# Expert rows by indirect DMA instead of by products with one-hot matrices

## The chip, the core and the metric

The program runs on one core of one Trainium2 chip. The metric is the device time of one execution in microseconds (us), lower being better. Engine names are those of the profile: PE (TensorE matmul), PEld (its weight load), DVE (VectorE), ACT (ScalarE), POOL (GpSimd), SP (SyncE); SPq and ACTq are the DMA issues of SP and ACT.

## What is computed

One transformer layer over 32 x 64 = 2048 rows of 128 elements: cross attention with a distance bias, then a mixture of 8 experts.

```python
x = x + xattn(layernorm(x), ctx, ctx, positions, ...)       # 16 heads of 8
xf = layernorm(x).reshape(-1, 128)
gate_logits = selu(xf @ gate_wi + gate_bi) @ gate_wo + gate_bo     # [2048, 128]
topv, topi = top_k(gate_logits, 2); topv = topv / topv.sum(-1)
onehot = (topi[..., None] == arange(8))                      # most of the 128 places name no expert
w = einsum('nk,nke->ne', topv, onehot)
h = selu(einsum('nh,ehf->enf', xf, exp_wi) + exp_bi)         # [8, 2048, 512]
out_e = einsum('enf,efh->enh', h, exp_wo) + exp_bo
x = x + einsum('enh,ne->nh', out_e, w)
```

The two chosen places are among 128, and only places 0 to 7 are experts, so that few rows have an expert at all.

## The kernel before

Rows lie in 16 tiles of 128 (`T`), in 4 groups of 4 (`TG`). Attention goes through the tiles. Then the second normalisation makes `XN2` (ACT `norm2`, DVE L889 for the last group; `inverse_std` on POOL, L383), and the gate goes through groups g and chunks c: PE `hidden(g, c)` (L1206), ACT exp and relu (L627, L628), DVE `SG` (L875), PE `logits(g)` (L1254), DVE adds, maxima and their places (L839 to L850). Each engine's order is written out by hand, and semaphores join the engines.

Beside that, every group of `XN2` is split into three bf16 parts that sum to the float32 value: ACT `first_part` (L584), POOL `rest2` (L402), ACT `second_part` (L588), POOL `last2` (L408). They go to `XW`, with three bf16 parts of the row's weights for the 8 experts and the membership (0 or 1) behind them.

The expert stage then works by products with one-hot matrices:

- DVE `choose` (L855) makes memberships and `Ub` (has the row any expert). PE counts (L1276 to L1278), and DVE turns counts into two loop bounds and ranks (L913 to L922).
- `pick_candidates` (L924) makes one-hots `G1` of up to 32 candidate rows of each tile. PE multiplies `XW` by `G1` (L1314) to give the candidates' rows and weights, `XC`, 4 blocks (`NC`) of 128.
- From prefix counts (`places`, L1294) comes `slot`: at which of the 128 places (`CAP`) of an expert a candidate stands. DVE makes the one-hots `G2` (L956), 4 x 1024 columns.
- PE multiplies `XC` by `G2` (L1324, 24 matmuls of 512 columns) for the transposed rows `XG` of all experts. Weights of the places come from L1379. `G1` and `G2` are transposed on PE (L1306, L1334) and copied out (L654, L965).
- For each expert PE `hidden(e)` (L1342), ACT and DVE selu (L677, L679, `selu` L967), PE `output(e)` (L1346): the expert's bias by one matmul (L1356) and four products (L1358; each float32 matmul shows as two records).
- Weighted outputs are split in three bf16 parts (`weigh` L661, `weigh_rest` L977). PE brings them back by `GT2` (`scatter`, L1362), DVE splits the sums again (L1010 to L1014), PE brings them to rows by `GT1` (L1403), DVE adds to `X` (L1019), and SP stores the four groups (L375).
- `expert_corrections` (L1235) makes a correction of the experts' bias rows: half of it right after the last logits, half after the counts.

The two loops around this run as often as the counts ask for; with these inputs each runs once.

Of the kernel before, what the change touches and what calls it, by code (L numbers as in the profile page):

```python
# [16 lines left out]
F32 = mybir.dt.float32  # L17
# [7 lines left out]
P = 128  # L25
# [5 lines left out]
CAND = 32  # L31
# [3 lines left out]
def build(nc, x, ctx_in, pos, Wq, bq, Wk, bk, Wv, bv, Wo, bo, emb, g_wi, g_bi, g_wo, g_bo, e_wi, e_bi, e_wo, e_bo, out):  # L35
# [23 lines left out]
    XWW = 3 * D + 4 * E  # L59
# [4 lines left out]
    with st:  # L64
# [6 lines left out]
        def sem(name):  # L71
            return st.enter_context(nc.semaphore(name))


        bins_dram = dram("bins_dram", [T, JB, IB, 2, L], BF16)
# [7 lines left out]
        ones_row = sb("ones_row", [2, P], F32)  # L83
# [12 lines left out]
        ebo_rows = sb("ebo_rows", [2, E, D], F32)  # L96
# [12 lines left out]
        ab = ExitStack()  # L109
        posq = sb("posq", [P, T, 3], F32, ab)  # L110
        posT = sb("posT", [T, P * 3], F32, ab)
        CX = XN2
        early = XW[:, :, :].rearrange("p t w -> p (t w)").bitcast(F32)
# [5 lines left out]
        w_att = sb("w_att", [P, 4, D], F32, ab)  # L119
        brow = ebo_rows[0:1, 0:5, :]  # L120
        bcols = sb("bcols", [P, 4], F32, ab)
        bo_b = sb("bo_b", [P, D], F32, ab)
# [5 lines left out]
        OH = sb("OH", [P, 2, IB * P], BF16, ab)  # L128
        bin_f = sb("bin_f", [P, 1], F32, ab)
# [25 lines left out]

        G1 = sb("G1", [P, T, P], BF16)
        GT1 = sb("GT1", [P, T, P], BF16)
        XC = sb("XC", [P, NC, XWW], BF16)
        OC = sb("OC", [P, NC, D], F32)
        OCr = sb("OCr", [P, NC, D], F32)  # L160
        OC3 = sb("OC3", [P, 3, NC, D], BF16)
        G2 = sb("G2", [P, NC, SLOTS], BF16)

        XN2T = sb("XN2T", [P, T * P], F32)
# [18 lines left out]
        GT2 = sb("GT2", [P, NC, E, P], BF16)  # L183
# [8 lines left out]
        Yr = sb("Yr", [P, 2, 2, D], F32)  # L192
        Y3 = sb("Y3", [P, 3, E, D], BF16)
# [6 lines left out]
        YB = [OPS, MPS, PTP[1], OPS]  # L200
        NY = len(YB)
        SCB = [PTP[0], SPS[0]]
        BKB = [SPS[1], SPS[2], SPS[3], SPS[0]]
# [5 lines left out]
        d_posq, oh_done, posq_tr, posq_done, bias_tr, perm_done, s_first, s_mm, pool_c, d_out = map(sem, (  # L209
            "d_posq", "oh_done", "posq_tr", "posq_done", "bias_tr", "perm_done", "s_first", "s_mm", "pool_c", "d_out"))  # L210
# [4 lines left out]
        xt_ev, q_ev, ge_done, d_gate, d_eb, d_ew, ao_tr, wo_mm = map(sem, (  # L215
            "xt_ev", "q_ev", "ge_done", "d_gate", "d_eb", "d_ew", "ao_tr", "wo_mm"))
        aot_ev, sub_done, exp_done, pv_mm, p_tr, pt_ev, n2_tr, n2_ev = map(sem, (
            "aot_ev", "sub_done", "exp_done", "pv_mm", "p_tr", "pt_ev", "n2_tr", "n2_ev"))
        consts2, h_mm, sg_done, cnt_done, xc_mm, xc_ev, g1_tr, xg_mm = map(sem, (
            "consts2", "h_mm", "sg_done", "cnt_done", "xc_mm", "xc_ev", "g1_tr", "xg_mm"))  # L220
        xg_ev, g2_tr, gt2_ev, eh_mm, se_done, he_done, dve_c = map(sem, (
            "xg_ev", "g2_tr", "gt2_ev", "eh_mm", "se_done", "he_done", "dve_c"))
# [4 lines left out]
        hr_done, y_mm, yb_done, y3_done, sc_mm, xw_done, eb_mm, eb_row = map(sem, (  # L227
            "hr_done", "y_mm", "yb_done", "y3_done", "sc_mm", "xw_done", "eb_mm", "eb_row"))
        mem_mm, mem_ev, y0_done, yr_done, gt1_ev, g1_zero, vs_done = map(sem, (
            "mem_mm", "mem_ev", "y0_done", "yr_done", "gt1_ev", "g1_zero", "vs_done"))  # L230
        w3_done, f_done, gb_mm, gb_ready, back_mm, rsum_done, stats_done, rstd_done = map(sem, (
            "w3_done", "f_done", "gb_mm", "gb_ready", "back_mm", "rsum_done", "stats_done", "rstd_done"))
        var2_done, shift_done, p0_done, p1_done, x2r_done, pool_const, dve_const, d_late = map(sem, (
            "var2_done", "shift_done", "p0_done", "p1_done", "x2r_done", "pool_const", "dve_const", "d_late"))
        WARM, IDENT, PART, KEYS, VD_ONES, NOUGHT, CONSTS = range(1, 8)
        VD_ZERO, BIASES, WQ_SCALED, BD_READY = 1, 2, 3, 3 + JB
        oc3_done = [sem(f"oc3_done{half}") for half in range(2)]
# [6 lines left out]
        x_back = [sem(f"x_back{q}") for q in range(NC)]  # L244
# [16 lines left out]
        out_dram = out.rearrange("b l d -> (b l) d").rearrange("(t p) d -> p t d", p=P)  # L261
# [19 lines left out]
        def _(sp):  # L281
# [69 lines left out]
            for t in range(4, T):  # L351
# [15 lines left out]
                if t == 2 * TG + 1:  # L367
                    sp.dma_start(ebi[:, :, :], e_bi.rearrange("e (c p) -> p e c", p=P), allow_slow_non_contiguous=True).then_inc(d_eb, 16)
                    sp.dma_start(ebo_rows[1:2, :, :], e_bo.rearrange("(a e) h -> a e h", a=1)).then_inc(d_eb, 16)

            sp.wait_ge(cnt_done, 1)
            outer = sp.value_load(cnt_i[0:1, 0:1], min_val=1, max_val=P // CAND)
            for g in range(NG):
                sp.wait_ge(x_back[g], outer)
                sp.dma_start(out_dram[:, tiles(g), :], X[:, tiles(g), :]).then_inc(d_out, 16)  # L375
            sp.wait_ge(d_out, 16 * NG)

        @block.gpsimd
        def _(pool):
# [18 lines left out]

            def rest2(g):

                pool.wait_ge(p0_done, g + 1)
                nc.gpsimd.tensor_tensor(x2r[:, :, :], XN2[:, tiles(g), :], XW[:, tiles(g), 0:D], ALU.subtract).then_inc(x2r_done, 1)  # L402

            def last2(g):

                pool.wait_ge(x2r_done, g + 1)
                pool.wait_ge(p1_done, g + 1)
                nc.gpsimd.tensor_tensor(XW[:, tiles(g), 2 * D:3 * D], x2r[:, :, :], XW[:, tiles(g), D:2 * D], ALU.subtract).then_inc(xw_done, 1)  # L408
                pool.wait_ge(xw_done, g + 1)
# [34 lines left out]
            link(nc.gpsimd.memset(ones_row[:, :], 1.0 / SELU_SCALE))  # L444
# [15 lines left out]
            pool.wait_ge(mv2_done, T)  # L460
            nc.gpsimd.memset(G1[:, :, :].rearrange("p t n -> p (t n)").bitcast(F32), 0.0).then_inc(g1_zero, 1)
# [7 lines left out]
            w3 = [XW[:, :, 3 * D + s * E:3 * D + (s + 1) * E] for s in range(3)]  # L469
# [3 lines left out]
            nc.gpsimd.tensor_tensor(w3[2], Wr[:, :, :], w3[1], ALU.subtract).then_inc(w3_done, 1)  # L473

        @block.scalar
        def _(act):
# [105 lines left out]
            def first_part(g):  # L582
                act.wait_ge(n2_done, g + 1)
                nc.scalar.activation(XW[:, tiles(g), 0:D], XN2[:, tiles(g), :], ACT.Copy).then_inc(p0_done, 1)  # L584

            def second_part(g):
                act.wait_ge(x2r_done, g + 1)
                nc.scalar.activation(XW[:, tiles(g), D:2 * D], x2r[:, :, :], ACT.Copy).then_inc(p1_done, 1)  # L588

# [6 lines left out]
            for t in range(T):  # L596
# [14 lines left out]
                if t in (TG + 2, 2 * TG + 2, T - 1):  # L611
                    norm2(t // TG - 1)
                    first_part(t // TG - 1)
                if t in (TG + 3, 2 * TG + 3):
                    second_part(t // TG - 1)
# [4 lines left out]
            for g in range(NG):  # L620
                for c in range(FC):
# [9 lines left out]
                    if c == FC - 2 and g < NG - 1:  # L631
                        evac_n2(g + 1)
                    if g == 0 and c == FC - 1:
                        second_part(NG - 2)

                if g == 1:
                    first_part(NG - 1)
                if g == 2:
                    second_part(NG - 1)
# [788 lines left out]
```

## Time and profile before

| | us |
|---|---|
| median of 3 runs | 216.96 |
| lowest and highest run | 215.62, 220.72 |
| profiled execution | 216.22 |
| its span, first to last instruction | 214.5 |

The profile is of one execution, so sums are made against its span of 214.5, which lies 1.72 us under that execution's own time. Attention takes roughly the first 128 us of the span, the gate the time to about 163, and the expert stage the rest. A timeline row gives start, length, engine, line, operation, output<-input, shape and count; brackets give the idle time of the engine before the row and what ended it.

### The profile page before, as it was taken

What the parts mean: (1) busy time and instruction counts of PE and PEld (TensorE: products, weight loads), DVE (VectorE), ACT (ScalarE), POOL (GpSimd) and SP (SyncE); (2) the same over time, 40 slices, a digit from 0 to 9 for tenths busy, and PEclk for the clock granted to TensorE, in tenths of its full rate; (3) what the DMA queues carried; (4) which work ended last, traced back from release to release, by engine and by line L of the source; (5) the groups of instructions that cost most, each with busy time, mean ns of one, the idle gap of its engine ahead of it and who ended that gap; (6) DMA issues with size and microseconds to landing.
All of it is one profiled execution on the core that took longest, in us unless ns stands there. A gap on an engine that the chain in (4) does not pass through costs nothing.

```text
span 214.5 us, 6218 instructions
## 1 busy us (share of the span) xinstructions
PE 185.8 (87%) x2516; PEld 139.5 (65%) x2517; DVE 160.7 (75%) x409; ACT 112.9 (53%) x225; POOL 43.8 (20%) x59
## 2 busy tenths in 40 slices
PE   2788839887999999999999997999995799999961
PEld 2355518475977767777777754758770449988951
DVE  6489995899977796779687735666899755788484
ACT  3278863543344376436744689597701245876100
POOL 7353998000000204020302001420303200000000
PEclk9999996999699999999999999999999999999999
DMA  5983599218994878996000000000000000000006
GB/s 137 261 206 105 115 361 394 76 38 280 286 314 128 255 137 212 367 392 218 3 3 3 3 0 0 2 5 0 2 0 0 3 0 3 2 3 2 0 3 196
DMA packets 28005, 24.20 MB, mean 113 GB/s; under 512 B 8628, under 2 KB 22215, under 8 KB 27976
## 3 DMA queue, kind: packets, MB, share of 16 engines
q1 hardware_dynamic: 25944, 23.01, 35.9%
q10 hardware_dynamic: 2032, 0.79, 1.4%
q8 instruction: 20, 0.33, 0.6%
q14 instruction: 9, 0.07, 0.1%
HBM read 17.24 MB, written 1.31 MB: 86 GB/s over the span
## 4 chain that ended last, share of the span: by engine, by line
PE 44%; DVE 30%; ACT 11%; issue 6%; POOL 3%; DMA 2%; SPq 1%; DVEq 1%; ACTq 0%; POOLq 0%
PE pair L1122 8%; PE pair L1136 6%; PE pair L1161 5%; PE pair L1149 5%; PE pair L1358 4%; PE pair L1342 4%; DVE mx L810 3%; DVE PR L813 2%; ACT GR L628 2%; ACT GE L627 2%; PE pair L1324 2%; DVE i L850 2%; PE pair L1368 2%; DMA ebo_rows<-in_L_xattn_bv_dram 2%; ACT PR L598 2%
## 5 line engine op out<-in xcount | busy, mean ns | idle before, releaser
L1122 PE MATMUL pair<-BD,OH 128*128 128x64 bf16 x768 | 27.3, 199 | 3.1 <-DVE OH L728 2.7
L1122 PEld LDWEIGHTS pair<-BD,OH 128*128 128x128 bf16 x768 | 26.7, 102 | 4.8 <-DVE BD L802 3.5
L598 ACT ACTIVATE PR<-PR 128x1024 f32<-128x1024 f32 x16 | 16.9, 1056 | 24.1 <-DVE PR L813 24.1
L605 ACT ACTIVATE PT<-pair 128x512 f32<-128x512 f32 x32 | 17.5, 595 | 16.9 <-PE pair L1149 16.8
L810 DVE TENSOR_REDUCE mx<-pair 128x16 f32<-128x1024 f32 x16 | 19.3, 1208 | 3.1 <-PE pair L1136 3.0
L1136 PE MATMUL pair<-KD,QT 64*64 64x256 f32 x256 | 21.4, 409 | 0.1
L383 POOL TENSOR_TENSOR rstd<-vare,half_neg 128x4 f32<-128x4 f32 x8 | 9.0, 1131 | 60.9 <-DVE vare L762 51.5
L1161 PEld LDWEIGHTS pair<-VD,PT 128*64 128x64 f32 x512 | 16.3, 138 | 6.3 <-issue 6.3
L813 DVE TENSOR_TENSOR PR<-pair,mx 128x1024 f32<-128x1024 f32 x16 | 19.6, 1224 | 0.5
L1149 PE MATMUL pair<-ident,PR 128*128 128x128 f32 x128 | 17.4, 280 | 2.7 <-ACT PR L598 2.3
L1149 PEld LDWEIGHTS pair<-ident,PR 128*128 128x128 f32 x128 | 14.3, 142 | 5.8 <-ACT PR L598 5.0
L1161 PE MATMUL pair<-VD,PT 128*64 128x18 f32 x512 | 17.9, 212 | 0.0
L875 DVE SCALAR_TENSOR_TENSOR SG<-GE,GR 128x512 f32<-128x512 f32 x16 | 10.8, 690 | 6.5 <-ACT GR L628 6.4
L1206 PE MATMUL pair<-XN2T,w_gi 128*128 128x512 f32 x32 | 15.0, 599 | 0.6 <-ACT XN2T L594 0.6
L1254 PE MATMUL pair<-w_go,SG 128*128 128x128 f32 x128 | 15.0, 276 | 0.5 <-issue 0.5
L1254 PEld LDWEIGHTS pair<-w_go,SG 128*128 128x128 f32 x128 | 14.7, 192 | 1.1 <-issue 1.1
L740 DVE TENSOR_TENSOR X<-X,pair 128x128 f32<-128x128 f32 x16 | 4.6, 286 | 14.3 <-PE pair L1175 14.2
L627 ACT ACTIVATE GE<-pair,gb_exp 128x512 f32<-128x512 f32 x16 | 11.4, 711 | 4.4 <-DVE SG L875 4.4
L728 DVE TENSOR_SCALAR OH<-BB,bin_id 128x2048 bf16<-128x2048 bf16 x16 | 13.2, 829 | 0.0
L628 ACT ACTIVATE GR<-pair,gbi 128x512 f32<-128x512 f32 x16 | 11.5, 716 | 0.0
L677 ACT ACTIVATE he<-pair,eb_exp 128x128 f32<-128x128 f32 x32 | 9.2, 374 | 4.3 <-PE pair L1342 4.3
L402 POOL TENSOR_TENSOR x2r<-XN,XW 128x512 f32<-128x512 f32 x4 | 4.6, 1162 | 32.0 <-ACT XW L584 32.0
(201 smaller groups left out, 352.0 us busy)
## 6 DMA issues: line engine op xcount, KB each, us to landing
BB<-bins_dram SPq DMA_DIRECT2D x16, 512.0 KB, 6.8
KD<-x2r SPq DMA_DIRECT2D x2, 2048.0 KB, 10.3
w_ei<-in_L_ffn_exp_wi_dram SPq DMA_DIRECT2D x8, 256.0 KB, 5.9
w_eo<-in_L_ffn_exp_wo_dram SPq DMA_DIRECT2D x8, 256.0 KB, 7.0
w_ei<-in_fside_BxSx_dram SPq DMA_DIRECT2D x8, 192.0 KB, 4.5
X<-in_x_dram SPq DMA_DIRECT2D x4, 256.0 KB, 6.4
KD<-KT SPq DMA_DIRECT2D x32, 32.0 KB, 2.5
out_dram<-X SPq DMA_DIRECT2D x4, 256.0 KB, 2.9
```

Of the source, the lines that this page charges most:

```text
L598: nc.scalar.activation(PR[:, t % 2], PR[:, t % 2], ACT.Exp).then_inc(exp_done, 1)
L605: nc.scalar.activation(PT[:, t % 2, 4 * half:4 * half + 4, :].rearrange("p c n -> p (c n)"), PTP[half][:, :], ACT.Copy).then_inc(pt_ev, 1)
L627: nc.scalar.activation(GE[:, n % 2, :], SPS[n % 4][:, :], ACT.Exp, bias=gb_exp[:, c:c + 1])
L628: nc.scalar.activation(GR[:, n % 2, :], SPS[n % 4][:, :], ACT.Relu, bias=gbi[:, c:c + 1]).then_inc(ge_done, 1)
L810: link(nc.vector.reduce_max(mx[:, t % 2], rows, AX.XY))
L813: nc.vector.tensor_tensor(PR[:, t % 2].rearrange("p h (i k) -> p h i k", i=2), rows, mx[:, t % 2].unsqueeze(2).unsqueeze(3).broadcast_to([ ...
L1122: mm(o, OH[:, t % 2, i * P:(i + 1) * P], BD[:, s], start=(i8_ == 0 and s == 0), stop=False, skip_group_check=True)
L1136: last = mm(SPS[two + ih][b2 * L:(b2 + 1) * L, r * JH * L // 2:(r + 1) * JH * L // 2], QT[rows, g, q0:q0 + L], KD[rows, g % KBUF, :, q0 + ...
L1149: last = tr(PTP[half][:, c * P:(c + 1) * P], PR[:, t % 2, 2 * cc:2 * cc + 2, :].rearrange("p h k -> p (h k)"), ident[:, :])
L1161: last = mm(OPS[b2 * L:(b2 + 1) * L, c * VW:(c + 1) * VW], PT[:, t % 2, c, b2 * L:(b2 + 1) * L], VD[:, 2 * t + b2, c, :], start=True, stop ...
L1206: mm(SPS[n % 4][:, :], w_gi[:, c * P:(c + 1) * P], XN2T[:, GTOK * g:GTOK * (g + 1)], start=True, stop=True).then_inc(h_mm, 1)
L1254: last = mm(o[:, u * D:(u + 1) * D], SG[:, g % 2, c, u * P:(u + 1) * P], w_go[:, c, :], start=(c == 0), stop=(c == FC - 1))
```

## The change

- The normalised rows `XN2` are stored to a DRAM tensor `x2_dram` as soon as each group is made. The rows after attention, `X`, are stored to the output early too, group by group. Both from SP, in the time of attention and gate.
- The bf16 parts of the rows and their four helpers are gone. `XW` now holds 3 parts of the weights, 2 labels (partition number, 128 times the tile number) and the membership.
- Ranks and slots of non-members are not sent far away but behind the members (`turn`, `minus_bf`, `past`), so that every one of the 128 places of an expert names a different row, of weight 0 if it is no member.
- `G2` is made in four batches of two experts (`pick_slots`). After each, PE sums weights and labels of the places (`sums_of_slots`), and DVE makes the row numbers (`rows_of_slots`, `row_i`).
- POOL fetches each expert's 128 rows of 512 bytes with an indirect DMA from `x2_dram` to `XR`; PE transposes them (`rows_transposed`); ACT or DVE copies them to `XG`.
- Each expert's weighted output goes by an indirect DMA that adds, from `Yw` to the output in DRAM. POOL waits for each of these eight before it issues the next.
- All transposes of one-hots, `scatter`, L1403 and L1019 are gone. The bias matmul has 128 rows in place of 2 (the others zero), and the bias corrections stand between the slot batches.

```diff
-            for g in range(NG):
-                sp.wait_ge(x_back[g], outer)
+            for g in range(NG):
+                sp.wait_ge(n2_done, g + 1)
+                sp.dma_start(x2_dram.rearrange("(t p) d -> p t d", p=P)[:, tiles(g), :], XN2[:, tiles(g), :]).then_inc(d_rows, 16)
+                sp.wait_ge(x2_done, TG * (g + 1))
                 sp.dma_start(out_dram[:, tiles(g), :], X[:, tiles(g), :]).then_inc(d_out, 16)
...
             for g in range(NG):
                 pool.wait_ge(var2_done, g + 1)
                 inverse_std(g)
-                rest2(g)
-                last2(g)
...
+            with pool.Fori(0, outer) as ro:
+                with pool.Fori(ro * inner, ro * inner + inner) as k:
+                    for b in range(NB2):
+                        pool.wait_ge(rows_done, k * NB2 + b + 1)
+                        pool.sem_inc(pool_seen, 1)
+                        for e in range(EB * b, EB * b + EB):
+                            pool.indirect_dma_start(XR[:, e, :], None, x2_dram, bass.IndirectOffsetOnAxis(row_i[:, e:e + 1], 0),
+                                                    bounds_check=B * L - 1).then_inc(d_xr[e], 16)
+                    for e in range(E):
+                        pool.wait_ge(y_done, k * E + e + 1)
+                        pool.sem_inc(pool_seen, 1)
+                        pool.indirect_dma_start(out_rows, bass.IndirectOffsetOnAxis(row_i[:, e:e + 1], 0), Yw[:, e, :], None,
+                                                bounds_check=B * L - 1, compute_op=ALU.add).then_inc(d_scat, 16)
+                        pool.wait_ge(d_scat, k * (16 * E) + 16 * (e + 1))
+                        pool.sem_inc(pool_seen, 1)
...
 # ACT, in the inner loop, ahead of the experts
+                    for b in range(2):
+                        act.wait_ge(xr_tr, k * NB2 + b + 1)
+                        nc.scalar.activation(XG[:, b * EB * CAP:(b + 1) * EB * CAP], PTP[0][:, 0:EB * CAP], ACT.Copy).then_inc(xg_ev, 1)
...
 # DVE
+            link(nc.vector.tensor_tensor(rank[:, :], rank[:, :], MPS[:, T * E + 2 * T:T * E + 3 * T], ALU.mult))
-                olink(nc.vector.memset(OC[:, :, :], 0.0))
+                    for b in range(NB2):
+                        pick_slots(b)
+                        rows_of_slots(b)
...
+                    for e in range(2, E):
                         selu(e)
+                        weigh(e - 2)
+                        if e in (2, 4):
+                            evac_xg(1 + e // 2)
+                    weigh(E - 2)
+                    weigh(E - 1)
+                    dve.wait_ge(d_scat, k * (16 * E) + 16 * E)
+                dve.wait_ge(xc_mm, ro + 1)
                 pick_candidates()
...
 # PE
-            expert_corrections(0)
...
+                    sums_of_slots(0)
+                    expert_corrections(0)
+                    sums_of_slots(1)
+                    expert_corrections(1)
+                    sums_of_slots(2)
+                    sums_of_slots(3)
+                    rows_transposed(0)
                     hidden(0)
                     hidden(1)
+                    rows_transposed(1)
                     for e in range(2, E + 2):
                         if e < E:
                             hidden(e)
+                        if e in (2, 4):
+                            rows_transposed(1 + e // 2)
                         output(e - 2)
```

The new `rows_of_slots(b)` is three DVE instructions on 2 experts (a sum of labels, a cast to integers, a sum of weights), and `weigh(e)` is one DVE multiplication of 128x128 from PSUM into `Yw`, which releases `y_done`.

## Rows read from the trace of the kernel before

**Rows 1.** Page, busy time of each engine, and the chain that ended last.
```profile
PE 185.8 (87%) x2516; PEld 139.5 (65%) x2517; DVE 160.7 (75%) x409; ACT 112.9 (53%) x225; POOL 43.8 (20%) x59
PE 44%; DVE 30%; ACT 11%; issue 6%; POOL 3%; DMA 2%; SPq 1%; DVEq 1%; ACTq 0%; POOLq 0%
```

**Rows 2.** Windows: stretch, length, PE, PEld, DVE, ACT, POOL busy, PEclk, DMA.
```profile
178.45:201.10 22.65, 22.63 (x220) 20.67 (x221) 16.33 (x42) 14.72 (x54) 0.00 (x0) 1.00 0.01 2
204.45:214.50 10.05, 3.67 (x60) 3.15 (x57) 6.91 (x18) 0.00 (x0) 0.00 (x0) 1.00 0.36 104
```

**Rows 3.** Chain that ended last, one expert's turn: start, us, what.
```profile
184.75 0.89 PE pair L1342 x8
185.65 0.41 PE pair L1356 x2
186.06 1.09 PE pair L1358 x8
```

**Rows 4.** Timeline, the end of the span.
```profile
201.11 0.62 ACT L668 ACTIVATE Y<-pair,wsl 128x128 bf16<-128x128 f32 x2 [3.67 <-PE pair L1358]
208.98 2.34 SPq L375 DMA_DIRECT2D out_dram<-X  x4
210.98 0.89 DVE L927 TENSOR_TENSOR G<-rank,slot_iota 128x128 bf16<-128x128 f32 x4 [0.23 <-DVE X L1019]
```

**Rows 5.** Timeline, gate: last norm, last logits, memberships.
```profile
134.45 1.16 POOL L408 TENSOR_TENSOR XW<-x2r,XW 128x512 bf16<-128x512 f32 x1 [4.79 <-ACT XW L588]
136.80 1.12 DVE L889 TENSOR_SCALAR XN<-X,mv,rstd 128x128 f32<-128x128 f32 x4 [2.09 <-POOL rstd L383]
155.90 3.81 PE L1254 MATMUL pair<-w_go,SG 128*128 128x128 f32 x32 [0.46 <-issue]
163.39 0.29 DVE L864 TENSOR_REDUCE Ub<-XW 128x16 bf16<-128x128 bf16 x1
```

**Rows 6.** Timeline, ranks and slots.
```profile
168.03 0.48 DVE L944 MEMSET OC<- 128x512 f32 x1 [0.17 <-PE pair L1291]
168.55 0.19 DVE L946 CAST memc<-pair 128x32 bf16<-128x32 f32 x1
168.80 0.23 PE L1298 MATMUL pair<-memc,ones_bf 128*128 128x24 bf16 x3 [0.45 <-DVE memc L946]
169.57 4.63 DVE L956 TENSOR_TENSOR G<-slot,slot_iota 128x1024 bf16<-128x1024 f32 x4 [0.21 <-DVE slot L951]
```

**Rows 7.** Timeline, from the slots to the first expert.
```profile
177.34 1.09 ACT L659 ACTIVATE XG<-pair 128x512 f32<-128x512 f32 x2 [3.06 <-PE pair L1324]
178.47 1.16 PE L1342 MATMUL pair<-XG,w_ei 128*128 128x128 f32 x8
179.47 0.98 PE L1379 MATMUL pair<-XC,G 128*128 128x3 bf16 x32
179.67 1.14 ACT L677 ACTIVATE he<-pair,eb_exp 128x128 f32<-128x128 f32 x4 [1.25 <-PE pair L1342]
182.24 0.69 DVE L974 SCALAR_TENSOR_TENSOR SE<-he,hr 128x512 f32<-128x512 f32 x1
```

**Rows 8.** Output tensor by tile, and POOL's rest of rows by line: landing, duration.
```profile
DMA to landing us min/median/max: 2.4/2.9/3.3
L402 POOL TENSOR_TENSOR x2r<-XN,XW x4: 1158/1162/1165, 80.8 to 142.4; 128x512 f32<-128x512 f32 x4
```

**Rows 9.** DMA issues: output<-input, queue, count, KB each, us to landing.
```profile
bins_dram<-binv ACTq DMA_DIRECT2D x2, 32.0 KB, 2.2
```

**Rows 10.** Windows and PE timeline around an idle PE; columns as above.
```profile
30.00:32.00 2.00, 0.00 (x0) 0.00 (x0) 1.93 (x7) 0.66 (x2) 1.83 (x3) 1.00 1.05 409
34.00:35.00 1.00, 1.00 (x9) 0.24 (x9) 1.00 (x3) 0.00 (x0) 1.00 (x1) 0.50 1.05 385
32.34 1.66 PE L1122 MATMUL pair<-BD,OH 128*128 128x64 bf16 x48 [2.72 <-DVE OH L728]
```

**Rows 11.** Groups by form, 162 to 178.4: busy us, mean ns, idle before.
```profile
L1239 PE MATMUL pair<-w_eo,neg_alpha 128*1 128x512 f32 x4 | 1.9, 591 | 0.0
L1291 PE MATMUL pair<-XW,G 128*128 128x8 bf16 x16 | 0.6, 167 | 1.5 <-DVE G L927 1.5
```

More of the change, by code:

```diff
@@ L58, in build @@
     NC = T * CAND // P
-    XWW = 3 * D + 4 * E
+    XWW = 6 * E
+    MEMB = 5 * E
+    SUMS = 5
+    EB = 2
+    NB2 = E // EB
     MAXRI = T * CAND // CAP
@@ L443, in _ @@
             nc.gpsimd.memset(neg_alpha[:, :], -SELU_ALPHA)
-            link(nc.gpsimd.memset(ones_row[:, :], 1.0 / SELU_SCALE))
+            link(nc.gpsimd.memset(ones_row[:, :], 0.0))
+            link(nc.gpsimd.memset(ones_row[0:2, :], 1.0 / SELU_SCALE))
             nc.gpsimd.memset(ones_row[0:1, :], 1.0)
@@ L468, in _ @@
             link(nc.gpsimd.tensor_tensor(Wt[:, :, :], we[:, 0], we[:, 1], ALU.add))
-            w3 = [XW[:, :, 3 * D + s * E:3 * D + (s + 1) * E] for s in range(3)]
+            w3 = [label(s) for s in range(3)]
             link(nc.gpsimd.tensor_copy(w3[0], Wt[:, :, :]))
@@ L632, in _ @@
                         evac_n2(g + 1)
[L633 to L639, printed above, removed]
-            for i in range(2):
-                act.wait_ge(eb_mm, i + 1)
-                nc.scalar.activation(ebo_rows[0:1, 4 * i:4 * i + 4, :].rearrange("a e h -> a (e h)"), SPS[2 + i][0:1, :], ACT.Copy).then_inc(eb_row, 1)
             act.wait_ge(consts2, 2)
@@ L680, in _ @@
                         last.then_inc(he_done, 1)
-                        if e % 2 == 1 and e >= 3:
-                            weigh((e - 3) // 2)
-                    weigh(NY - 1)
         @block.vector
@@ L997, in _ @@
                     dve.wait_ge(wsl_done, k + 1)
[L998 removed]
                     selu(0)
[L1000 to L1001 removed]
+                    selu(1)
+                    for e in range(2, E):
                         selu(e)
[L1003 to L1014 removed]
@@ L1301, in places @@
                        skip_group_check=True).then_inc(slot_mm, 1)
-                def g1_transposes(half):
-                    pb = PTP[half][:, :].bitcast(BF16)
-                    for u in range(T // 2):
-                        last = tr(pb[:, u * P:(u + 1) * P], G1[:, half * (T // 2) + u, :], ident_bf[:, :])
-                    last.then_inc(g1_tr, 1)
-                g1_transposes(0)
                 places()
@@ new lines, in _, with sums_of_slots @@
+                    pe.wait_ge(xc_ev, ro + 1)
+                    def sums_of_slots(b):
+                        pe.wait_ge(g2_done, k * NB2 + b + 1)
+                        if b >= 2:
+                            pe.wait_ge(rows_done, k * NB2 + b - 1)
+                        for u in range(EB):
+                            e = EB * b + u
+                            for q in range(NC):
+                                last = mm(RB[b % 2][:, SUMS * u:SUMS * u + SUMS], G2[:, q, e * CAP:(e + 1) * CAP],
+                                          XC[:, q, e:MEMB:E], start=(q == 0), stop=(q == NC - 1))
+                        last.then_inc(ws_mm, 1)
@@ L1337, in hidden, with rows_transposed @@
+                    def rows_transposed(b):
+                        if b >= 1:
+                            pe.wait_ge(xg_ev, k * NB2 + b)
+                        for u in range(EB):
+                            pe.wait_ge(d_xr[EB * b + u], k * 16 + 16)
+                            last = tr(PTP[0][:, u * P:(u + 1) * P], XR[:, EB * b + u, :], ident[:, :])
+                        last.then_inc(xr_tr, 1)
                     def hidden(e):
+                        pe.wait_ge(xg_ev, k * NB2 + e // EB + 1)
+                        if e in (2, 3):
+                            pe.wait_ge(eb_row, k * 2 + e - 1)
```

312 lines of the change are left out of this document (113 added, 199 removed).

## The prediction

> **What bounds the kernel now.** I began with the page. PE is busy 87% of the span and holds 44% of the chain that ended last, DVE 75% and 30% [rows 1]. DMA appears with 2%: nothing in the second half waits for memory. The page mixes three stages, so I went to the windows of the last one. From 178.45 to 201.10 PE works 22.63 of 22.65 us [rows 2]: the experts are bound by PE. Their turn is 0.89 + 0.41 + 1.09 = 2.39 us on the chain (hidden layer, bias, output) [rows 3]. The tail, 204.45 to 214.5, is the opposite: DVE 6.91 of 10.05 us, PE 3.67 [rows 2]. It is the split of sums, the way back by one-hots, the addition to X, and stores issued from 208.98 on [rows 4]. Between memberships (163.68) and the first expert (178.47) lies a chain of DVE and PE in turn [rows 5 to 7]. The change touches these three parts and a little of the gate.
>
> **The change part by part.** I rebuild the times of each new step, starting from the point in the trace that releases it.
>
> *Early stores.* Eight stores of 256 KB leave between the norms and about 140 us. SP's loads are all issued before them, it then has nothing to do until the counts, and one such store lands in 2.9 us [rows 8]. I cost them at nothing: the last is covered by the gate, some 20 us of it. Without that cover they would cost POOL about 3 us, since its loop waits for them.
>
> *Gate.* POOL's split of a group (1.16 us, begun at 134.45) stands before the last `inverse_std`; DVE waited 2.09 us for it before the norm at 136.80 [rows 5]. Without it SG, GE and GR run some 2 us earlier, but PE is nearly gapless there, and 0.5 to 1.3 us is what passes through to the last logits (155.90) and `Ub` (163.39). ACT loses eight copies of about 0.65 us as well, which only feed the same chain. I take 1.0 us; bounds 0 (PE is bound anyway) and 2.1.
>
> *Counts and slots.* Added: one linked DVE multiplication for ranks, 0.2, and one for slots, 0.2. Removed: the 0.48 us memset, behind which `memc` waited. `places` has 11 small matmuls after `memc` where 4 took about 0.27 us, so 0.45 more [rows 6]. Slots were ready for `G2` at 169.57; now 169.57 - 1.0 + 0.4 - 0.5 + 0.4 = 168.9.
>
> *Slots to first expert.* Before, `G2` took 4.63 us in four instructions [rows 6], the 24 products ran beside it to 177.5 and the copy of `XG` to 178.4 [rows 7]. Now there are four rounds in series on DVE: one quarter of `G2`, 1.22; 8 of the 32 small products, 0.98 / 4 = 0.25 [rows 7], with a handover to PE and back, 0.3; three small DVE instructions of 0.18, linked, 0.6 in all. Sum 2.3 to 2.4, four of them 9.3: row numbers of the last batch at 178.1. PE has its sums done 0.8 earlier, at 177.3. Two transposes (0.35) and a copy of 256 columns (0.4) give `hidden(0)` at 178.1, against 178.47 [rows 7]. Three savings (24 products, the wide L1314, the transposes of one-hots) are thus nearly all eaten by the DVE rounds. The bias corrections (1.9 us each, [rows 11]) stand on PE in rounds 1 and 2 behind a pick of 1.22 us, and cost little at full clock.
>
> *TensorE's clock.* This cover may go. PE was empty for 2.72 us before the bias products at 32.34, and its granted clock fell from 1.00 to 0.50, 1.2 GHz in place of 2.4, at 34 us and stayed there some 3 us [rows 10]. In the changed kernel the first bias correction no longer fills the gap after the last logits: PE is empty about 4 us before the counts and 3.6 us after them. I therefore expect half clock into the corrections: each then takes about 3.7 us, and the pick no longer covers it. That is 1.5 us more until `hidden(0)`; bounds 0 and 3. I take 1.5, since the gaps are longer than the one shown.
>
> *Gathers.* Indirect DMAs don't occur in this trace. For POOL's part of one I take its nearest row, an operation on 128 partitions: 1.16; for the transfer a store of the output, 2.9 [rows 8]. Row numbers of a batch come every 2.3 us and feed two gathers, 2.3 us of POOL: it just keeps up. Two rows of the first batch are then there at 176.3 (needed 177.3), of the second at 178.6 (needed 180), of the third at 180.9 (needed 181.9). Hidden, with 1 us to spare; their cost is 0 up to a POOL share of about 1.5 us each.
>
> *Experts.* ACT copies two batches of `XG` before its first exponential, and the second batch is transposed behind `hidden(1)`. The first exponential moves from 179.67 [rows 7] to 180.9. The first selu ends at 184.0 in place of 182.93, then PE's turn of 2.39 runs on [rows 3] with three pairs of transposes, 0.3 each, and without the first `scatter` (1.3). The bias matmul with 128 rows instead of 2 shows the same columns; I cost it at 0 to 0.2. DVE multiplies output 0 after selu 2, at 187.9; outputs 1 to 7 are ready about 189.9, 192.5, 194.7, 197, 200, 200.3 and 201.6. With the clock's 1.5 us, output 0 is ready at 189.4 and the last at 203.1.
>
> *Adding DMAs.* Here is the price that decides. The eight are in series by POOL's own wait: each is issue, read of the destination, write, completion. From below a turn can't be under 2.2 us, the quickest small store that the hardware queue made [rows 9]. From above: 1.16 for POOL, 2.9 for a read leg and 3.3 for the slowest store [rows 8], 7.4. I take 1.16 + 2.9 = 4.06, since a row of 512 bytes is small and the read leg should be partly inside, while software issue is not. So 189.4 + 8 x 4.06 = 221.9. Behind the last one DVE waits, picks candidates again (0.89 [rows 4]), and loops and program end: together 1.75. Span 223.6.
>
> *The Trainium skill on this price.* "DMA: Bandwidth & Descriptors", section "Anatomy of one DMA — SWDGE (gpsimd) path", gives about 2.0 us plus the bytes over 436 GB/s for a DMA issued from GpSimd. For 64 KB that is an estimate of 2.15 us, and eight in series would end before the experts do. The trace has no DMA from POOL to hold against it; its own stores of 256 KB land in 2.4 to 3.3 us. "SBUF — State Buffer", section "Who interferes with whom", says that some two-port DVE instructions lock GpSimd out while they run, which would speak for longer turns; no row here shows it.
>
> *The sum.* Tail before: from the last output product (201.1) to 214.5, 13.4 us. Tail now: from the last output (203.1) to 223.6, 20.5. Start of the experts' outputs about 2 us later, made of the clock and the copies. Net 223.6 - 214.5 = +9.1 us. The profiled execution took 216.22, so 225.3; the median lies 0.74 above it, which gives 226.
>
> **The rivals.** The forecast, F: the series of adding DMAs sets the end with turns of about 3.5 us or more. For it: the wait in POOL's loop, and that DMAs of a kind lighter than these already need 2.2 to 3.3. Against it: only a turn's length, unmeasured.
>
> A: the same series, turns of 2.4 to 3.4 us. With 3.0: 189.4 + 24 + 1.75 = 215.2, or 217.6 as a median: no change. Break-even with 214.5 is (214.5 - 1.75 - 189.4) / 8 = 2.9 us (3.1 if the clock stays). For it: stores land in 2.9 with their issue. It needs software issue and the read of the destination to cost next to nothing.
>
> B, on the other side: the series hides under the experts. Outputs come every 2.2 to 2.6 us; a turn below that keeps up, and only the last three lie open, since outputs 5, 6 and 7 are ready within 1.6 us. With 2.2: 201.5 + 6.6 + 1.75 = 209.9, without the clock's loss 208.4; median 211 to 212, 2.5% faster. It decides below 2.4 us. The skill's figure would make it so, by its page named above. For it, the tail of 13.4 us is truly gone; against it, it needs the lowest row of the trace for a heavier operation.
>
> C: POOL is slow at making indirect DMAs, over 2.5 us each. Then gathers come late too: two per round make 5 us against 2.3 supplied, so the fourth expert's rows arrive about 4 us late and PE stands, and turns are 5.5 us or more. 193 + 44 + 1.75 = 239, median 241. For it: nothing in the trace bounds POOL's share from above but this kernel's need.
>
> That the change does nothing can't be: L1324, L1403 and L1019 are gone from the program.
>
> **How the numbers follow.** F 0.58, A 0.22, B 0.12, C 0.08. The price of a turn moves the time by 8 times its error, and nothing else comes near: gate 1 us, clock 1.5 us. The measured difference is meaningful from about 2%, 4.3 us: under 212.6 is faster, over 221.3 slower. With a turn of 3.46 us the median would be 221.3. So slower is F and C, 0.66; same is A, 0.22; faster is B, 0.12. The likeliest is 226. The range takes turns from 2.3 to 5.6 us: 212 to 239, which leaves out most of B and C. F's own range is 221 to 236.
>
> **What would show each step.** The output's adding DMAs back to back on POOL, each released by the one before: the series holds; their spacing is the price. POOL waiting for DVE's `weigh` between them: B. PE idle before `rows_transposed` with the DMA as releaser: C. Granted clock at 0.50 between 163 and 176, and bias corrections of twice 1.9 us: the clock's step. DVE rounds 2.3 us apart and `hidden(0)` near 178 to 180: the slot step. The last norm near 134.7: the gate step. The prediction is wrong if a turn is under 3.4 us, or if something other than the last adding DMA ends last.

## The result, and the profile after

The changed kernel takes 226.41 us (median of 4 runs, 225.95 to 228.47), beside 216.38 us for the kernel before on the same chip. The ratio is 1.049, with an interval of 1.042 to 1.057: slower, and 0.4 us from the predicted 226. Some executions of one and the same kernel are disturbed and take longer; the ratios here and below are of undisturbed runs alone (all four of this kernel, 3 of 6 of `corrections_back`, 3 of 4 of `corr_copy_filled`, 3 of 12 of `fetch_filled`).

The profiled execution took 226.27 us, 224.5 of it span, 10.0 more than the span before. Parts of its page, in its order: busy time, the granted clock in 40 slices, the chain that ended last, and the groups of the two new operations (busy us, mean ns, idle before).

```profile
PE 170.1 (76%) x2320; PEld 127.7 (57%) x2320; DVE 150.9 (67%) x397; ACT 102.3 (46%) x204; POOL 61.1 (27%) x75
...
PEclk9999988999999999999999999999956959995555
...
PE 36%; DVE 26%; DMA 17%; issue 9%; ACT 7%; POOL 2%; SPq 1%; DVEq 0%; POOLq 0%; ACTq 0%
...
L493 POOL DMA_INDIRECT out_dram<-Yw,row_i x8 | 12.5, 1568 | 25.0 <-issue 13.5
...
L488 POOL DMA_INDIRECT XR<-x_dram,row_i x8 | 9.8, 1220 | 7.1 <-issue 6.5
```

The view of DMA issues (queue, count, median us to landing) of the changed kernel has the two as well:

```profile
XR<-x_dram,row_i POOLq DMA_INDIRECT x8, 2.6
out_dram<-Yw,row_i POOLq DMA_INDIRECT x8, 3.3
```

PE lost 15.7 us of work against [rows 1] and DVE 9.8, and the kernel is slower by 10. DMA went from 2% to 17% of the chain: one part of the program now waits for memory (12% of the chain are the adds, `out_dram<-Yw,row_i`). The windows (stretch, length, then PE, PEld, DVE, ACT, POOL busy, granted clock, DMA share, GB/s) say which:

```profile
176.00:178.10 2.10, 0.65 (x11) 0.42 (x11) 1.31 (x5) 0.38 (x1) 1.80 (x1) 1.00 0.11 31
178.10:201.50 23.40, 21.02 (x150) 19.47 (x150) 13.65 (x36) 13.36 (x49) 8.81 (x7) 0.85 0.15 23
201.50:222.70 21.20, 0.00 (x0) 0.00 (x0) 0.00 (x0) 0.00 (x0) 7.79 (x5) 0.53 0.17 15
```

The experts take 23.4 us where they took 22.65 [rows 2]. Then come 21.2 us in which PE, DVE and ACT do nothing at all; the old tail of [rows 2] had DVE at work for 6.9 of 10 us. POOL's timeline (start, duration, in brackets the idle time before and what ended it) shows what fills them:

```profile
189.14 1.64 POOL L493 DMA_INDIRECT out_dram<-Yw,row_i  x1 [6.07 <-DVE Yw L983]
193.53 1.56 POOL L493 DMA_INDIRECT out_dram<-Yw,row_i  x1 [2.75 <-DVE Yw L983]
197.77 1.56 POOL L493 DMA_INDIRECT out_dram<-Yw,row_i  x1 [2.68 <-issue]
202.02 1.56 POOL L493 DMA_INDIRECT out_dram<-Yw,row_i  x1 [2.69 <-DVE Yw L983]
206.41 1.56 POOL L493 DMA_INDIRECT out_dram<-Yw,row_i  x1 [2.84 <-issue]
210.61 1.56 POOL L493 DMA_INDIRECT out_dram<-Yw,row_i  x1 [2.64 <-issue]
214.81 1.56 POOL L493 DMA_INDIRECT out_dram<-Yw,row_i  x1 [2.64 <-issue]
219.09 1.56 POOL L493 DMA_INDIRECT out_dram<-Yw,row_i  x1 [2.72 <-issue]
```

Eight starts, 4.20 to 4.39 us apart. Where DVE's `Yw` stands as the releaser, this name misleads: the output for the add at 202.02 was ready at 195.3 (the fourth `Yw`), 6.7 us earlier. What ended the wait was the landing of the add before. The chain that ended last says so, here over one turn (start, duration, what):

```profile
189.14 3.36 DMA out_dram<-Yw,row_i
192.50 0.02 issue
192.52 0.02 POOLq L497
...
192.79 0.52 issue
...
193.53 3.22 DMA out_dram<-Yw,row_i
```

A turn is 3.2 to 3.4 us from POOL's start to landing (the 1.56 us of POOL lie inside), and then 1.0 us until POOL starts the next one. The last add starts at 219.09 and lands at 222.49; DVE picks candidates at 222.76, where in [rows 4] it was released by its own addition to X at 210.98. The timeline names what it waited for:

```profile
222.76 0.90 DVE L916 TENSOR_TENSOR G<-rank,slot_iota 128x128 bf16<-128x128 f32 x4 [21.28 <-DMA out_dram<-Yw,row_i]
```

### The profile page after: what moved, and what is told of

Its sections match the earlier page's. It is cut to its first block, busy times and chain, and to the rows that moved or that the text cites. A ratio compares the mean times of both kernels' runs of the same rounds, so it can differ in the third digit from the quotient of the medians.

```text
span 224.5 us, 5872 instructions
## 1 busy us (share of the span) xinstructions
PE 170.1 (76%) x2320; PEld 127.7 (57%) x2320; DVE 150.9 (67%) x397; ACT 102.3 (46%) x204; POOL 61.1 (27%) x75
## 3 DMA queue, kind: packets, MB, share of 16 engines
q0 software_dynamic: 1408, 1.05, 3.5%
## 4 chain that ended last, share of the span: by engine, by line
PE 36%; DVE 26%; DMA 17%; issue 9%; ACT 7%; POOL 2%; SPq 1%; DVEq 0%; POOLq 0%; ACTq 0%
DMA out_dram<-Yw,row_i 12%; PE pair L1100 6%; PE pair L1184 5%; PE pair L1232 5%; PE pair L1114 4%; DVE mx L799 4%; PE pair L1139 4%; DMA BB<-bins_dram 4%; PE pair L1127 3%; PE pair L1217 2%; DMA b_rows<-in_L_xattn_bv_dram 2%; DVE PR L802 2%; DVE OH L717 2%; PE pair L1153 2%; DVE early L695 2%
## 5 line engine op out<-in xcount | busy, mean ns | idle before, releaser
L389 POOL TENSOR_TENSOR rstd<-vare,half_neg 128x4 f32<-128x4 f32 x8 | 9.6, 1194 | 99.6 <-DVE vare L751 90.4
L614 ACT ACTIVATE PR<-PR 128x1024 f32<-128x1024 f32 x16 | 16.9, 1057 | 25.1 <-DVE PR L802 25.1
L1100 PE MATMUL pair<-BD,OH 128*128 128x64 bf16 x768 | 26.3, 196 | 2.4 <-DVE OH L717 2.4
L1100 PEld LDWEIGHTS pair<-BD,OH 128*128 128x128 bf16 x768 | 25.6, 100 | 3.9 <-DVE BD L791 3.2
L1114 PE MATMUL pair<-KD,QT 64*64 64x256 f32 x256 | 21.2, 405 | 0.1
L493 POOL DMA_INDIRECT out_dram<-Yw,row_i x8 | 12.5, 1568 | 25.0 <-issue 13.5
L916 DVE TENSOR_TENSOR G<-rank,slot_iota 128x128 bf16<-128x128 f32 x8 | 2.1, 319 | 21.3 <-DMA out_dram<-Yw,row_i 21.3
L717 DVE TENSOR_SCALAR OH<-BB,bin_id 128x2048 bf16<-128x2048 bf16 x16 | 12.4, 778 | 2.2 <-DMA BB<-bins_dram 2.2
L488 POOL DMA_INDIRECT XR<-x_dram,row_i x8 | 9.8, 1220 | 7.1 <-issue 6.5
```

What stands on the lines that cost most here:

```text
L493: pool.indirect_dma_start(out_rows, bass.IndirectOffsetOnAxis(row_i[:, e:e + 1], 0), Yw[:, e, :], None, bounds_check=B * L - 1, compute_op ...
L614: nc.scalar.activation(PR[:, t % 2], PR[:, t % 2], ACT.Exp).then_inc(exp_done, 1)
L717: nc.vector.tensor_scalar(OH[:, t % 2, :], BB[:, t % 4, :], bin_id[:, 0:1], None, ALU.is_equal).then_inc(oh_done, 1)
L1100: mm(o, OH[:, t % 2, i * P:(i + 1) * P], BD[:, s], start=(i8_ == 0 and s == 0), stop=False, skip_group_check=True)
L1114: last = mm(SPS[two + ih][b2 * L:(b2 + 1) * L, r * JH * L // 2:(r + 1) * JH * L // 2], QT[rows, g, q0:q0 + L], KD[rows, g % KBUF, :, q0 + ...
```

## The experiments

Every kernel is the changed one with the edit shown. The first four ran on one chip beside the kernel before at 215.97 us, the others on a second one beside 217.02.

**Is it the dependence between the adds?** `own_targets` gives each expert a DRAM tensor of its own to add to, so that nothing has to wait.

```diff
-pool.indirect_dma_start(out_rows, ..., Yw[:, e, :], ..., compute_op=ALU.add).then_inc(d_scat, 16)
-pool.wait_ge(d_scat, k * (16 * E) + 16 * (e + 1))
+pool.indirect_dma_start(out_rows if e == 0 else own[e - 1], ..., Yw[:, e, :], ..., compute_op=ALU.add).then_inc(d_scat, 16)
 # after the loop over e:
+pool.wait_ge(d_scat, k * (16 * E) + 16 * E)
```

> The changed kernel with each expert's adding DMA going to a DRAM tensor of its own (expert 0 to the output, the others to copies of it that SP stores early), so that POOL needs no wait between the eight and waits once behind the last. The sum over experts is left out, so the output lacks experts 1 to 7. Theory (POOL's wait between dependent adds is the price): the DMAs leave as outputs become ready (the last at 201.5 in the changed kernel), 2 to 2.5 us apart, the last lands near 205.5, and the span falls from 224.5 to about 207. Rival (POOL's making of an adding DMA, or the DMA engines' work on it, is the price, wait or no wait): they stay about 4.2 us apart and the span stays within 1 us of 224.5.

It took 212.34 us in its single run; its span of 210.6 is 13.9 us under that of the changed kernel. 0.7 of them lie before `Ub` (161.04 against 161.73), which the edit does not concern. Its timeline, the last adds and what DVE waited for behind them:

```profile
196.93 1.55 POOL L496 DMA_INDIRECT own<-Yw,row_i  x1 [0.67 <-issue]
199.58 1.56 POOL L496 DMA_INDIRECT own<-Yw,row_i  x1 [1.09 <-DVE Yw L985]
201.59 1.56 POOL L496 DMA_INDIRECT own<-Yw,row_i  x1 [0.45 <-issue]
203.45 1.56 POOL L496 DMA_INDIRECT own<-Yw,row_i  x1 [0.30 <-issue]
205.32 1.56 POOL L496 DMA_INDIRECT own<-Yw,row_i  x1 [0.30 <-issue]
...
208.82 0.69 DVE L918 TENSOR_TENSOR G<-rank,slot_iota 128x128 bf16<-128x128 f32 x3 [6.51 <-DMA own<-Yw,row_i]
```

The adds now follow the outputs; where outputs are plentiful POOL issues one every 1.86 us, 1.56 plus a gap of 0.30. The last add lands no sooner than in the changed kernel: 3.23 us by the chain. So some 13 us are the price of the dependence, and not of eight adds as such. Whether the wait could be dropped while all eight add to one tensor is not shown: no run kept the one target without it. The span is 3.6 us above what I had written down: outputs came 0.8 us later in this execution, and the last three, ready within 2 us, queued at 1.86 us each, which I had left out.

**What is a turn made of?** `plain_store` keeps every wait and stores in place of adding; `quarter_rows` keeps the add and sends 32 of the 128 rows.

```diff
 # plain_store
-  bounds_check=B * L - 1, compute_op=ALU.add)
+  bounds_check=B * L - 1)
 # quarter_rows
-  IndirectOffsetOnAxis(row_i[:, e:e + 1], 0), Yw[:, e, :], ...
+  IndirectOffsetOnAxis(row_i[0:32, e:e + 1], 0), Yw[0:32, e, :], ...
```

> The changed kernel with its eight indirect DMAs storing instead of adding, POOL's waits kept. The addition is left out: rows named by an expert hold only its last output. Theory (the read of the destination is a leg of its own, about 0.7 us as estimated from 3.3 us to landing for adds against 2.6 for fetches of the same size): turns shrink from 4.28 to about 3.6 us and the span to about 219. Rival (issue and completion make the turn, the read is hidden): turns stay at 4.2 or more, the span at 224.

> The changed kernel with the eight adding DMAs taking only the first 32 of the 128 places of an expert, waits kept. The outputs of the other 96 places are left out. Theory (a turn is mostly fixed: wait, POOL's start, completion): POOL's 1.56 us shrink by at most 0.6 and a turn goes from 4.28 to 3.5 or more, span 218 to 222. Rival (a turn is made by the number of rows): a turn falls by over 1.5 us, span under 213.

`plain_store` took 219.97 us, `quarter_rows` 222.59, one run each. Two starts from the end of each POOL timeline, `plain_store` first:

```profile
210.65 0.98 POOL L493 DMA_INDIRECT out_dram<-Yw,row_i  x1 [2.29 <-issue]
213.92 0.98 POOL L493 DMA_INDIRECT out_dram<-Yw,row_i  x1 [2.29 <-issue]
```

and `quarter_rows`:

```profile
212.42 1.31 POOL L493 DMA_INDIRECT out_dram<-Yw,row_i  x1 [2.37 <-issue]
216.16 1.30 POOL L493 DMA_INDIRECT out_dram<-Yw,row_i  x1 [2.44 <-issue]
```

Over the whole series a turn is 3.36 us for a store ((213.92 - 190.42) / 7; 3.28 once the experts are done) and 3.78 for an add of a quarter of the bytes, against 4.28 for the add. So adding costs 0.9 to 1.0 us of a turn: 0.58 in POOL's own instruction (1.56 against 0.98), the rest in the transfer. Three quarters of the rows cost 0.5 us, half of it in POOL again. About 3.3 us remain for a plain indirect store of 128 rows that waits for the one before; a store of fewer rows was not run. Even adds of a quarter of the rows would have given back only 4 of the 10 us (8 x 0.50; the run was 3.7 us shorter). The pages of the profile also show that the DMA engines get more pieces for an add: 1408 packets on POOL's queue in the changed kernel, 512 in `plain_store`, 640 in `quarter_rows`, and 256 in `fetch_only`, which has the eight fetches alone. That makes 144 packets for an add, 48 for an add of 32 rows and 32 for a store or a fetch. Whether the packets make the difference in time is not shown.

**What did the clock and the order of the front cost?** `corrections_back` puts the bias corrections back behind the last logits and the counts, where they stood before the change.

```diff
             logits(NG - 1)
+            expert_corrections(0)
...
             # behind the matmuls of Ub
+            expert_corrections(1)
...
                     sums_of_slots(0)
-                    expert_corrections(0)
                     sums_of_slots(1)
-                    expert_corrections(1)
```

> The changed kernel, complete, with the two bias corrections back where the kernel before had them: one behind the last logits, one behind the counts. Theory (their place in the slot rounds and the clock that fell to 0.50 over the gaps cost the start of the experts): PE holds 1.00 from 160 to 178, the slot rounds are 2.15 us apart, the first expert starts 1.3 us earlier, at about 176.8, and the first two run at full clock; span 224.5 to about 221.5. Rival (the clock falls anyway, since PE is now nearly empty in the slot rounds): only the 1.3 us, span 223.

It took 226.56 us (median of 6), ratio 1.036 (1.028 to 1.045). The profiled execution was 4 us longer than the shortest of the six, so I compare stretches of it and not its end. Windows, columns as above:

```profile
166.00:168.00 2.00, 0.53 (x17) 0.42 (x17) 1.39 (x6) 0.59 (x1) 1.71 (x5) 1.00 0.00 0
170.00:172.00 2.00, 0.38 (x8) 0.29 (x8) 1.46 (x5) 0.00 (x0) 0.00 (x0) 0.50 0.00 0
178.00:180.00 2.00, 1.53 (x7) 1.20 (x6) 0.62 (x5) 0.38 (x1) 1.39 (x3) 0.50 0.14 37
```

The corrections ran at full clock (1.88 us for four matmuls). But the rounds of the slot step then held 0.38 us of PE's work in 2, and the clock stood at 0.50 in them and under the first hidden layers. Those took 3.78 us for 16 matmuls; at full clock 16 of the same take 2.05 (in `fetch_filled`, below). The fall was not avoided, only moved. From `Ub` to `hidden(0)` it is 15.2 us, against 16.4 in the changed kernel: 1.1 gained, which is what the rival of the expectation said. To the first add only 0.3 is left of it (27.1 against 27.4).

`corr_and_copy` adds to this that DVE and not ACT copies the second batch of `XG`.

```diff
-                    for b in range(2):
+                    for b in range(1):
                         act.wait_ge(xr_tr, k * NB2 + b + 1)
...
+                    evac_xg(1)
                     selu(0)
```

> Corrections back as before, and DVE instead of ACT copies the second pair of fetched experts. Theory (ACT's copy of the second pair stands before the first exponential and delays output 0, from which the series of adds counts): the first exponential starts right behind the first expert's hidden layer, 1.2 to 2 us sooner (3.6 us behind its start in the changed kernel, 1.2 here), the first add leaves about 1.5 us sooner, ratio to the kernel before about 1.030 against 1.036. Rival (PE's half clock and the first outputs set the start anyway): under 0.5 us, no difference.

225.39 us (median of 4), ratio 1.033 (1.026 to 1.040). The first exponential starts 2.1 us behind `hidden(0)` in place of 3.7, and from `Ub` to the first add it is 25.9 us against 27.4 in the changed kernel and 27.1 in `corrections_back`. The trace shows the step; the ratios of the two kernels are too close to show it.

`corr_copy_filled` keeps PE at work in the rounds with products that nobody reads.

```diff
+                filler(4)   # 4 bf16 products of 512 columns into SPS[1]
                 with pe.Fori(ro * inner, ro * inner + inner) as k:
...
-                    sums_of_slots(0) ... sums_of_slots(3)
+                    for b in range(NB2 - 1):
+                        sums_of_slots(b)
+                        filler(4)
+                    sums_of_slots(NB2 - 1)
```

> The same with matmuls that nobody reads (bf16, 128x512, into a free bank), four behind the candidates' products and four behind each of the first three slot sums, where PE waits for DVE. Theory (PE's emptiness in the slot rounds lets the granted clock fall to 0.50, and the first experts pay for it): clock 1.00 through the rounds and the experts, the first two hidden layers take 2.0 us instead of 3 to 3.8, outputs 1.5 to 2 us sooner; ratio about 1.022. Rival (the half clock is granted late and costs little beside the waits): same as without filler.

224.93 us (median of 4), ratio 1.028 (1.020 to 1.036). Three windows:

```profile
164.00:166.00 2.00, 2.00 (x4) 0.14 (x2) 1.78 (x12) 0.00 (x0) 1.78 (x5) 0.58 0.02 4
172.00:174.00 2.00, 1.24 (x12) 0.51 (x12) 1.47 (x5) 0.00 (x0) 1.62 (x2) 1.00 0.00 0
178.00:180.00 2.00, 2.00 (x10) 2.00 (x11) 0.26 (x2) 0.13 (x1) 1.70 (x2) 0.50 0.29 70
```

The clock was up in the later rounds (1.00 from 172 to 178), but it was at 0.58 from 164, at 0.50 from 166 to 170 and at 0.50 again from 178. From `Ub` to the first add 25.1 us, 0.8 less than without the fillers. The clock was not held, so the cost of half clock by itself is not isolated; what is shown is that all three repairs of the front together are worth 2.3 us up to the first add (27.4 to 25.1), and that the kernel stays 2.8% behind.

**Which half of the change loses?** `fetch_only` fetches the rows by indirect DMA as the changed kernel, with the repairs of `corr_and_copy`, but returns the outputs by products with one-hots and the addition to X, as the kernel before; so the transposes of one-hots are back in the rounds and the stores of the output at the end. The diff is shortened.

```diff
-for e in range(E):
-    pool.wait_ge(y_done, ...)
-    pool.indirect_dma_start(out_rows, ..., compute_op=ALU.add)
-    pool.wait_ge(d_scat, ...)
+# PE, behind the experts, as before
+for half in range(2):
+    scatter(NY - 1, half).then_inc(sc_mm, 1)
...
+# DVE: OC split in three parts, then
+nc.vector.tensor_tensor(X[:, tiles(q), :], X[:, tiles(q), :], BKB[q][:, :]..., ALU.add)
```

> One half of the change alone: rows come to the experts by indirect DMA, outputs go back by the one-hot products, the split sums and the stores of the kernel before (transposes of one-hots in the slot rounds, corrections back, second pair copied by DVE). Theory (the whole loss is on the way back; the fetch is hidden and the gate's split is saved): first expert near 177.2 against 178.47 before, last output 0.9 us more for three pairs of transposes, then the old tail of 13.4 us: span 213 to 215, ratio 0.99 to 1.00; with half clock in the first experts up to 1.01. Rival (the fetch side costs too: slot rounds, POOL): span above 218, ratio over 1.02.

214.72 us (median of 6, 213.79 to 216.36), ratio 0.989 (0.985 to 0.994): 1.1% faster than the kernel before, which is less than the 2% from which the prediction called a difference meaningful. By the quotient of the ratios it is 5.7% faster than the changed kernel, and 4.2% faster than `corr_and_copy`, which has the same repairs and ran on the same chip (medians 214.72 and 225.39, 10.7 us apart). The last output product ends at 198.57 and the span at 212.0: a tail of 13.4 us, as in the kernel before (201.1 to 214.5). Its end, from the chain:

```profile
198.57 3.36 PE pair L1432 x60
...
206.98 1.29 DVE X L1050 x2
...
208.56 0.17 DVE G L946
```

The profiled execution, the shortest of the six, is 2.5 us shorter than that of the kernel before (span 212.0 against 214.5). Two rows say where, with the row of the kernel before for the first of them (its `Ub` stands in [rows 5]):

```profile
132.43 0.17 DVE L762 TENSOR_SCALAR vare<-mv 128x4 f32<-128x4 f32 x1
130.58 0.17 DVE L781 TENSOR_SCALAR vare<-mv 128x4 f32<-128x4 f32 x1
160.72 0.29 DVE L883 TENSOR_REDUCE Ub<-XW 128x16 bf16<-128x128 bf16 x1
```

`vare` is the variance of the last group's rows, ahead of the last norm. 1.85 us of the 2.5 lie before it. In the nine kernels without the split of rows, `vare` comes anywhere from 129.86 to 133.43, so this trace can't put these 1.85 us down to the edit. From `vare` to `Ub` the kernel before takes 30.96 us and this one 30.14: the gate's step, 0.8. From `Ub` to the last output product it takes 37.85 us against 37.7: here fetching instead of multiplying gains nothing.

The way back is where the time goes. Behind the last output the changed kernel needs 23.0 us (201.5 to 224.5), this one 13.4. From `Ub` to the end `corr_and_copy` takes 61.3 us and this one 51.3. So adding DMAs in series cost some 10 us against the products.

`fetch_filled` adds three unread products after each of the first three rounds.

```diff
                         sums_of_slots(b)
                         g2_transposes(b)
+                        filler(3)
```

> The same with three unread matmuls behind each of the first three batches of slot sums and transposes. Theory: clock 1.00 through rounds and first experts, 1 to 2 us less than without, ratio 0.98 to 0.99. Rival: no difference, or 0.5 us more where a filler stands before a slot sum.

The median of its 12 runs is 214.92 us (211.15 to 218.31); the ratio of 0.978 (0.971 to 0.986) rests on the three shortest alone (211.15, 212.59, 213.92). The profiled one, span 210.6, shows the first hidden layers at full clock (window and PE's timeline):

```profile
174.00:176.00 2.00, 1.73 (x23) 1.33 (x22) 1.28 (x6) 1.41 (x3) 1.69 (x2) 1.00 0.06 14
175.58 2.05 PE L1399 MATMUL pair<-XG,w_ei 128*128 128x128 f32 x16
177.98 0.57 PE L1388 MATMUL pair<-ident,XR 128*128 128x128 f32 x2 [0.35 <-DMA XR<-x_dram,row_i]
```

With a quicker front fetches are awaited for the first time, two of them, by 0.35 and 0.45 us. With a median over all runs that nearly equals that of `fetch_only`, I take no gain from the fillers as shown.

## Why the prediction was right, step by step

**The end.** The series of adding DMAs sets it, F. Predicted: output 0 ready at 189.4, a turn of 4.06, the last landing at 221.9. Measured: 188.17, 4.29 on average ((222.49 - 188.17) / 8), 222.49. The misses are -1.2 us at the start and +1.8 over the eight turns, and they largely offset each other: that the median came within 0.4 us of the forecast is luck, while the series as what sets the end is not. The remainder of the program after the landing took 2.0 where I had 1.75. Span 224.5 against 223.6.

**The turn's parts.** The sum 1.16 + 2.9 was right in total and not in its parts, and that is luck too. Predicted were 1.16 us of POOL and then 2.9 of transfer. POOL takes 1.56, what follows it until landing 1.7 (3.3 - 1.6), and a third term was missing: 1.0 us on POOL's queue between a landing and the next start. Without it the measured parts give 3.3 us, which is rival A. That the read of the destination would hide inside was wrong too: adding costs 1.0 us (`plain_store`). The range of 2.2 to 7.4 was wide for a reason: no row of the kernel before had such a DMA in it, and the store of 32 KB at 2.2 us [rows 9] was half of the truth.

**The rivals.** A, turns of 2.4 to 3.4 us, is what `plain_store` is: 3.36 us a turn, for which the prediction's sum gives 220.5 (221.3 less 8 x 0.1), measured 219.97. The add itself lifts the turn from there to F's. B, the series hidden under the experts, is what `own_targets` nearly is, once nothing waits: 1.86 us a turn and a span 3.9 us under that of the kernel before (with the summing of the eight tensors left out). C is refuted: 1.0 to 1.8 us of POOL, not over 2.5. The Trainium skill, "DMA: Bandwidth & Descriptors", section "Anatomy of one DMA — SWDGE (gpsimd) path", whose figure gave the estimate of 2.15 us, does not hold here for an indirect add: the landing alone takes 3.3. The prediction's remark that a series at 2.15 us would end before the experts was wrong by its own numbers: no add can leave before its output is ready, and rival B has the last three lie open behind the experts. For a plain indirect store the landing of 2.2 to 2.6 us in `plain_store` is near it, but a turn in a series is 1.0 us longer than the landing.

**Gate.** Predicted -1.0, measured -1.7 at `Ub` (161.73 against 163.39 [rows 5]). DVE no longer waits for POOL before the last norm, which starts at 133.91 without idle time before it. About half of the gain is older: `vare`, on which that norm rests, came at 131.60 where it came at 132.43 before. As said, that time moves by 3.6 us among kernels that are alike up to there. From `vare` to `Ub` it is 30.13 us against 30.96, and 30.13 or 30.14 in all the other kernels without the split: the step is worth 0.8 us.

**Ranks and slots.** From `Ub` to `G2` 6.24 us against 6.18 [rows 5, 6]: +0.3 predicted, +0.06 measured.

**Rounds and clock.** Predicted four rounds of 2.3 and 1.5 us for half clock, `hidden(0)` at 178.1 + 1.5 = 179.6; measured 178.09. The rounds are 2.15 us, except the second, where the first correction (`169.55`, 3.19 us for four matmuls at 0.50 where [rows 11] has 1.9) keeps PE from the sums and DVE idle for 1.73. That round took 3.43 us (picks at 170.12 and 173.55), so the clock cost about 1.3 us up to `hidden(0)`, for the 1.5 of the forecast. The timeline:

```profile
169.55 3.19 PE L1217 MATMUL pair<-w_eo,neg_alpha 128*1 128x512 f32 x4
172.97 1.88 PE L1217 MATMUL pair<-w_eo,neg_alpha 128*1 128x512 f32 x4
173.08 0.16 DVE L955 TENSOR_REDUCE row_f<-pair 128x2 f32<-128x4 f32 x1 [1.73 <-PE pair L1306]
```

The step is right in kind; I had it hit both corrections, and it hit one. I did not forecast a second fall: after PE had been empty for 1.78 us before the last sums, the clock was at 0.50 again from 180 to 184, under the first hidden layers.

**Experts.** First exponential predicted 2.8 us behind `hidden(0)`, measured 3.7 (181.75). The excess is the second fall of the clock (16 matmuls of `hidden` took 2.92 us, at full clock 2.05). In `corr_and_copy`, without ACT's second copy, 2.1 are left. Last output predicted at 203.1, ready at 201.5, and it did not matter: its add began 17.6 us later.

**Gathers and early stores.** Hidden, as predicted: in the changed kernel nobody waits for `XR` by way of a DMA. POOL 1.0 us (predicted 1.16) where nothing disturbs it, landing 2.6 (2.9). The early stores land in 3.7 us at the median (2.9) and nothing waits for them.

## What to carry to other kernels

A chain of dependent DMAs costs its full latency each time, here 4.3 us with 1.0 of it before the DMA even starts, and still 3.8 with a quarter of the rows: count such a chain as links times latency, and look at how soon the links' inputs come. An indirect fetch whose addresses are early hides (here but for 0.8 us in the fastest kernel), so judge the two directions of such a change apart: here the way there was worth 0.8 us, in the gate, and the way back lost some 10. Before a gain of 1% is read from two traces, look at how far the part before the edit moves by itself. Before a gap is opened on TensorE, ask which work ran behind it at full clock.

## What the runs showed of the hardware

- An indirect DMA of 128 rows of 512 bytes costs POOL 1.0 us as a fetch or a store and 1.56 as an add where nothing disturbs it; of 32 rows as an add 1.3. Without waits, a fetch or an add follows 0.3 us behind the end of the one before. Landing takes 2.6 us for the fetch, 2.3 for the store and 3.3 for the add.
- POOL's fetches are longer when a large DVE instruction runs. From the timelines of `fetch_only`:

```profile
171.66 1.23 DVE L977 TENSOR_TENSOR G<-slot,slot_iota 128x1024 bf16<-128x1024 f32 x1
171.94 1.83 POOL L504 DMA_INDIRECT XR<-x_dram,row_i  x1 [0.30 <-DVE row_i L987]
173.81 1.23 DVE L977 TENSOR_TENSOR G<-slot,slot_iota 128x1024 bf16<-128x1024 f32 x1
174.08 1.84 POOL L504 DMA_INDIRECT XR<-x_dram,row_i  x1 [0.30 <-DVE row_i L987]
177.55 1.01 POOL L504 DMA_INDIRECT XR<-x_dram,row_i  x1 [0.30 <-issue]
```

  Both fetches end 0.88 us after the pick beside them (173.77 against 172.89, 175.92 against 175.04), as do those of the changed kernel begun at 174.30 and 175.96; alone one takes 1.01. It looks as if these fetches begin their work only when the pick is over. The first fetch of each kernel does not fit so well: in the changed one it ran 1.49 us from 171.06 and ended 1.2 us after its pick. The Trainium skill, "SBUF — State Buffer", section "A bandwidth-pool intuition that's wrong (but worth ruling out)", describes such a wait for a DMA issued from GpSimd that meets a DVE `tensor_copy`: it is blocked until that ends. The pick is a `tensor_tensor`, which the section does not speak of, so the agreement is one of kind; no run here varied the pick's form. It cost nothing, since the fetches had slack. The adds mostly don't show it: 1.56 us with DVE at work (193.53) as without (219.09), though one of `corrections_back` took 1.81 and two stores of `plain_store` 1.17 and 1.29 in place of 0.98 while the experts ran.
- TensorE's granted clock changed four times in 24 us of the changed kernel: 0.50 (1.2 GHz) from 162 to 172, behind a stretch in which PE was empty for 4.44 us; 1.00 (2.4 GHz) from 174 to 178, behind the two bias corrections; 0.50 from 180 to 184, behind the thin rounds; 1.00 from 186, behind the first hidden layers. Closing one gap moved the fall to the next in `corrections_back` and in `corr_copy_filled`.
